# Ordering an edge list by block only, and placing its words by indirect DMA instead of by one-hot products

## The reference

```python
x = _layernorm(x + L0(x, edge_index_t, 1250, W, b))        # relu(x[src] W1 + x[dst] W2 + b), summed over edges by src
x = _layernorm(x + L1(x, edge_index, edge_type_8, edge_weight, ...))  # attention over edges, summed by dst
x = _layernorm(x + L2(x, src, dst, deg, ...))               # mean of x[src] by dst, then two products
x = _layernorm(x + L3(x, edge_index, edge_type_2, basis1, att1, ...)) # two gated layers, summed by src
```

## Time and profile before

| | |
|---|---|
| time of the runs | 2698.16 us median of 3 (2689.44 to 2699.32) |
| profiled execution, first to last instruction | 2541.8 us; its whole time is not recorded apart, the median is 156.4 us above this span |
| PE busy | 1969.9 us (78%) |
| DVE busy | 1458.9 us (57%) |
| POOL busy | 976.5 us (38%) |
| ACT busy | 479.5 us (19%) |
| DMA over the span | 336.66 MB, mean 132 GB/s |
| mean granted clock of PE | 0.883 |

### The profile page before, as it was taken

The page is one execution under the profiler, slowest core; times in us unless marked ns, Lnnn a source line. Parts: engine busy times, 40 slices in busy tenths (PEclk is TensorE's granted clock), DMA queues, the critical chain, the costliest instruction groups (busy, mean ns, idle before and its releaser), DMA issues. The chain is left out here.

```text
span 2541.8 us, 36616 instructions
## 1 busy us (share of the span) xinstructions
PE 1969.9 (78%) x8289; PEld 1126.0 (44%) x8290; DVE 1458.9 (57%) x3550; ACT 479.5 (19%) x889; POOL 976.5 (38%) x974
## 2 busy tenths in 40 slices
PE   7767695885989998558287775699867998888884
PEld 6633385564545554347144442233333333343331
DVE  5644467675257776687677777444453444204445
ACT  4101130111135554223200002100044000120000
POOL 0000000001047771440078773477700777207773
PEclk9988755998989999755599998899989999999998
DMA  0079700998046663000166670577712777317775
GB/s 16 0 160 212 157 0 21 205 206 214 32 117 193 186 191 74 26 0 0 50 176 172 173 183 28 174 208 210 196 36 95 236 209 207 102 66 206 209 208 143
DMA packets 99747, 336.66 MB, mean 132 GB/s; under 512 B 19744, under 2 KB 20369, under 8 KB 95851
## 3 DMA queue, kind: packets, MB, share of 16 engines
q0 software_dynamic: 71904, 235.41, 33.2%
q1 hardware_dynamic: 24714, 96.39, 14.9%
q10 hardware_dynamic: 3072, 4.20, 0.8%
HBM read 310.83 MB, written 25.10 MB: 132 GB/s over the span
## 5 line engine op out<-in xcount | busy, mean ns | idle before, releaser
L658 PE MATMUL e_pS<-e_rows,e_onehot_ring 128*128 128x512 f32 x1408 | 689.4, 617 | 179.9 <-issue 59.7
L578 POOL DMA_INDIRECT e_rows<-tab_y,e_idx_ring x352 | 334.8, 951 | 332.7 <-ACT e_idx_ring L638 226.1
L658 PEld LDWEIGHTS e_pS<-e_rows,e_onehot_ring 128*128 128x128 f32 x1408 | 246.4, 192 | 480.8 <-issue 404.6
L610 DVE TENSOR_TENSOR acc<-e_pS,acc 128x512 f32 x352 | 242.6, 689 | 377.1 <-PE e_pS L658 373.9
L578 POOL DMA_INDIRECT e_rows<-tab_h,e_idx_ring x176 | 205.0, 1165 | 208.1 <-ACT e_idx_ring L638 158.5
L968 PE MATMUL n_pY<-weights,n_xT_block 128*128 128x512 f32 x560 | 260.1, 615 | 0.0
L1583 POOL DMA_DIRECT2D a_in<-in_L_gnn_a_src x1 | 1.0, 966 | 611.0 <-POOLq L43 611.0
L578 POOL DMA_INDIRECT e_rows<-tab_n,e_idx_ring x176 | 167.7, 953 | 77.2 <-issue 49.9
L717 POOL DMA_INDIRECT e_rows<-tab_q,e_idx_ring x176 | 169.8, 965 | 68.1 <-issue 46.4
L792 PE MATMUL e_pS<-e_rows,e_onehot_f 128*128 128x512 f32 x352 | 166.6, 597 | 0.0
L968 PEld LDWEIGHTS n_pY<-weights,n_xT_block 128*128 128x128 f32 x560 | 107.5, 199 | 118.3 <-issue 118.3
(11 more groups left out here) (309 smaller groups left out, 3077.4 us busy)
## 6 DMA issues: line engine op xcount, KB each, us to landing
basis_piece<-in_L_gnn_basis SPq DMA_DIRECT2D x128, 480.0 KB, 11.8
tab_y<-n_y_ring SPq DMA_DIRECT2D x40, 256.0 KB, 2.2
e_rows<-tab_y,e_idx_ring POOLq DMA_INDIRECT x352, 3.7
tab_w<-basis_wout ACTq DMA_DIRECT2D x128, 32.0 KB
w_raw<-in_L_gnn_W SPq DMA_DIRECT2D x3, 1024.0 KB, 10.1
weights<-tab_w SPq DMA_DIRECT2D x3, 1024.0 KB, 5.8
e_rows<-tab_q,e_idx_ring POOLq DMA_INDIRECT x176, 3.7
e_rows<-tab_h,e_idx_ring POOLq DMA_INDIRECT x176, 3.8
```

Of the source, the lines that this page charges most:

```text
L578: pool.indirect_dma_start(rows[:, q, s, :], None, table, bass.IndirectOffsetOnAxis(idxr[:, half, n:n + 1], 0)).then_inc(got[q], 16)
L610: nc.vector.tensor_tensor(a, pS[:, u % 4, :], a, ALU.add).then_inc(added, 1)
L658: ins = nc.tensor.matmul(pS[:, u % 4, :], ohr[:, u % 4, s, :], rows[:, u, s, :], start=s == 0, stop=s == 1)
```

## The change

The source list alone is treated anew; the destination list is sorted and placed as before, by `sort_edges` (now without its third stage) and `place_edges` (that third stage as a function of its own, unchanged, with the tiles `pos_p`, `pos_s` and `value` passed in).

```diff
-            sort_edges(nc, "src", C, identb, f(SRC), [(f(DST), 1 << SH1), (f(REL1), 1 << SH2)], None,
-                       pairs["src"][:, :], blocks["src"][:, :], [packed["src"][:, :]], basis[1])
-            sort_edges(nc, "dst", C, identb, f(DST), [(f(SRC), 1 << SH1), (f(T8), 1 << SH2)], f(WT),
-                       pairs["dst"][:, :], blocks["dst"][:, :], [packed["dst"][:, :], weight[:, :]], basis[0])
+            pos_p, pos_s, value = (sb(n, [EP, T], F32)[:, :] for n in ("pos_partition", "pos_slot", "packed_value"))
+            bucket_edges(nc, "src", C, f(SRC), [(f(DST), 1 << SH1), (f(REL1), 1 << SH2)],
+                         pairs["src"][:, :], blocks["src"][:, :], pos_p, pos_s, value)
+            scatter_edges(nc, "src", C, pos_p, pos_s, value, dram("slots_src", [P * SLOTS, 1]), packed["src"][:, :], basis[1])
+            sort_edges(nc, "dst", C, identb, f(DST), [(f(SRC), 1 << SH1), (f(T8), 1 << SH2)],
+                       pairs["dst"][:, :], blocks["dst"][:, :], pos_p, pos_s, value)
+            place_edges(nc, "dst", C, pos_p, pos_s, value, f(WT), [packed["dst"][:, :], weight[:, :]], basis[0])
```

More of the change, by code:

```diff
@@ L234, in store, with sort_edges @@
             act.wait_ge(self.stored[k], self.STEPS * 64)
-def sort_edges(nc, name, C, identb, key, packed, extra, pair_block, block_f, sorted_out, basis=None):
-    values = [0] if extra is None else [0, 1]
+def sort_edges(nc, name, C, identb, key, packed, pair_block, block_f, pos_p, pos_s, value):
     with ExitStack() as ctx:
@@ L262, in sort_edges @@
         eqtmp = sb("eq_tmp", [EP, 4, EP], F32)
-        pos_p, pos_s = sb("pos_partition", [EP, T], F32), sb("pos_slot", [EP, T], F32)
-        value = sb("packed_value", [EP, T], F32)
         with ExitStack() as c1:
@@ L455, in _ @@
                 peeled(pe, T // GT // 2, step)
[L459 to L465, removed]
-            if basis:
[L467 to L517, removed]
@@ new lines, in scatter_edges, with _, step @@
+def scatter_edges(nc, name, C, pos_p, pos_s, value, slots, sorted_out, basis):
+    with ExitStack() as ctx:
+        sb = lambda n, s, d: ctx.enter_context(nc.sbuf_tensor(f"{name}_{n}", s, d))
+        sem = stage_semaphores(nc, ctx, name)
+        at = sb("slot_row", [EP, T], I32)
+        empty = sb("empty", [P, SLOTS], F32)
+        basis.begin(ctx, sem)
+        cleared, addressed, emptied, placed, read_back = (
+            sem("cleared"), sem("addressed"), sem("emptied"), sem("placed"), sem("read_back"))
+        block = ctx.enter_context(nc.Block())
+        by_part = slots.rearrange("(p s) a -> p (s a)", s=SLOTS)
+        @block.sync
+        def _(sp):
+            basis.load(sp)
+        @block.scalar
+        def _(act):
+            basis.store(act)
+        @block.vector
+        def _(v):
+            basis.clear_mix()
+            nc.vector.memset(empty[:, :], 0.0).then_inc(cleared, 1)
+            nc.vector.scalar_tensor_tensor(at[:, :], pos_p, float(SLOTS), pos_s, ALU.mult, ALU.add
+                                           ).then_inc(addressed, 1)
+        @block.gpsimd
+        def _(pool):
+            pool.wait_ge(cleared, 1)
[8 more added lines that the diff above has]
+            pool.wait_ge(read_back, 16)
+        @block.tensor
+        def _(pe):
+            basis.start_multiply(pe)
+            def step(i):
+                for k in range(2):
+                    basis.multiply(pe, i, k)
+            peeled(pe, Basis.STEPS, step)
```

115 lines of the change are left out of this document (111 added, 4 removed).

## The result

The change makes the kernel slower, by 0.6%: 2707.68 us median of 10 runs (2703.04 to 2714.21) against 2691.24 (2685.13 to 2702.54) of before, a ratio of 1.0058, 95% interval [1.0042, 1.0074]. Forecast were 2631.2 us and a range of 2590 to 2700. The profiled execution took 2704.2 us, its span 2701.9.

What follows compares the result with a forecast made beforehand. Stages follow one another across barriers, so a change is worth what it does to its own stage's length. Sorting -106.6 and placing +39.6 give -67.0 us: 2698.2 becomes 2631.2 us, range 2590 to 2700.

Steps and rivals of the forecast that it cites:

- Sort stage: Source list's sort: 126.75 us go, a DVE chain of 20.1 us takes their place, a saving of 106.6 us.
- The doubt about strides: Source list's sort: were the strided reduction and two strided products twice as slow, 26 us instead of 20.1.
- The rival of an unshortened stage: Source list's sort not shortened, through far slower strided operations; it would take 80 us more than 20; chance 0.03.
- The placing stage: Placing of the source list: POOL's chain of scatters takes 212.3 us against 172.7, or +39.6.
- I take 1.25, since a scatter too is one index for each partition: Placing of the source list: 160 scatters start 1.25 us apart, like gathers of 128 rows, 200 us in all.
- The upper bound of the text: Placing of the source list: scatters priced like gathers from `tab_h`, made while DVE multiplies rows, 1.47 us each, 235 us.
- This costs nothing if POOL may run ahead: Placing: scatters slowed to 4.4 us beside basis loads cost nothing; POOL issues all in 200 us, the rest drains behind.
- Hidden: Placing: without the 0.30 us of issue, scatters take 164 us under the basis work; 2592 us; chance 0.12.
- The engines become the bound: Placing: basis's 161 us plus 1250 words at 0.06 us make 248 us; 2667 us in all; chance 0.18.
- the cover of 0.034: Placing: POOL's pace of 200 us covers a cost of 0.034 us a word on a DMA engine.
- POOL held by a full queue: Placing: scatters slowed beside loads, the rest following at 1.25 us; 2708 us at 2.4 us each, 2746 at 4.4; chance 0.17.
- The list's order: Later gathers by the source list, whose rows now come in ascending destination order with repeats: costed at nothing.

Runs made afterwards that it cites:

- block order alone: The change with the source list's words placed by one-hot products instead of scatters: 2426.34 us, ratio 0.9561 to before; in a later job 2592.73 us, 0.9605.
- e2: Not a run but a later pass of the kernel; in the trace of before its 176 gathers of 128 rows show no gap above 0.31 us.
- the waits after 13: The change with POOL made to wait, after every 13 scatters, until all issued have landed: 2743.26 us (before: 2693.56 us in that job).
- 128-row version: The change with scatters of 128 rows instead of 125, the extra words going to spare places behind the table: 2486.41 us, ratio 0.979; in another job 2740.11 us, 1.0152.
- e0: Not a run but a pass of the kernel that gathers by the source list; its gathers of 128 rows stop before the 114th.

## Why the prediction was wrong

**Sort stage.** Right. 126.75 became 21.23 us, a saving of 105.5 where 106.6 was forecast. The doubt about strides was in place, but small. Two reductions of the kernel after:

```profile
22.77 2.83 DVE L513 TENSOR_REDUCE src_bucket<-src_in_bucket 125x160 f32<-125x1600 f32 x1
...
28.05 1.92 DVE L523 TENSOR_REDUCE block_of_pair_src<-src_pair_at_least 128x88 f32<-128x792 f32 x1
```

They were costed at 2.14 and 1.1 us. Both read with a stride and add up few terms for each result (10 and 9), and no run parts the two. The rival of an unshortened stage falls.

**The placing stage** was forecast at 212.3 us and took 294.8. By the forecast's own terms:

| term | forecast | measured | off |
|---|---|---|---|
| start to the first scatter | 4.0 | 3.2 | -0.8 |
| 160 scatters at their pace | 160 x 1.25 = 200 | 160 x 1.485 = 237.6 | +37.6 |
| POOL standing still | 0 | 50.1, less 4 x 0.3 of usual gap | +48.9 |
| last landing, read-back, barrier | 8.3 | 5.3 | -3.0 |

The measured is 34.06 less 30.91 for the start and 325.70 less 320.4 for the end. The terms sum to +82.7; 82.5 is what is to be explained.

**The first failed step is "I take 1.25, since a scatter too is one index for each partition".** The gap of 0.30 us was right to the hundredth, but POOL's own part is 0.97 us at 128 rows, 1.18 at 125 and 1.31 at 124. It rises with the words of a packet (8, 25 and 31, as worked out above), though not in proportion, and the gather from which the price came had 128 rows. The upper bound of the text, 1.47 us from the gathers of `tab_h`, was nearly the value, for another reason. By an estimate, at 1.485 us and with no stop the stage would have been 294.8 - 48.9 = 245.9 us, 73.2 above that of before, and the kernel 105.5 - 73.2 = 32.3 us faster.

**The second is "This costs nothing if POOL may run ahead".** It may for 39 scatters of 125 rows and for 113 of 128, and there are 160. The forecast has 0 us for POOL standing still, a term that no row and no run shows; with 125 rows the profile showed 50.1 us in four stops, and even with 128 rows POOL stopped once, for 12.96 and 20.37 us beside loads (206 to 210 GB/s until 155 us). The nine plain DMAs of the earlier trace rows were too few to show it, as the prediction said itself, but the trace of before had the row at 883.81 us, a stop of 1.95 us before the 114th gather, and the prediction did not use it.

**Rivals.** *Hidden* is refuted: the gap of 0.30 us stands throughout. *The engines become the bound* is refuted: scattering alone, from 275 to 320 us, the share is 0.07 at one scatter in 1.49 us, so a word costs, by an estimate from these, 0.07 x 16 x 1.49 / 125 = 0.013 us, under the cover of 0.034. The scatters did slow the loads: PE's last basis product ends at 217.3 us, 186.4 after the stage's start, where it took 167.7 before (305.1 - 137.4). These 19 us are not on the path, since POOL works 103 us longer. *POOL held by a full queue* was right in kind, and its 2708 us is by chance the result; its mechanism was not. It had POOL held at the engines' pace all through the loads. In fact POOL goes at its own pace and then stands still, which fits a wait until what is in flight has landed: with idle engines a stop of 2.3 us is the 1.6 to 1.7 us of a plain wait for landing and 0.65 more. The price of being held was 48.9 us, where the rival's 2708 us contained 289 - 212 = 77; the dearer scatter made up the rest.

**Costed at nothing.** The list's order is right by the block order alone. That PE's longer idle time costs the destination sort nothing is also a term that no row of before shows; it is right by the run, with 124.30 us at a granted clock of 0.50 against 124.05 at 0.51. The 156.4 us between span and median were wrongly taken for time around the span, but carried over unchanged they did no harm to the difference.

What is open: why the gathers of e2 and of `tab_y` run past 113 without a stop, and why a landing beside 16 KB packets costs 9.5 us and 0.35 us a scatter. With 8 KB packets the stops after 39 are 9.08 and 10.0 us instead of 20.23 and 23.14, and a backlog that only grows by the scatter would have made the waits after 13 a third of those after 39, which were 21.19 and 24.28 us where the waits were 12.6 to 15.0. How the DMA engines divide their time between the queues no run shows.

## What to carry to other kernels

Before replacing compute by many small DMAs, ask whether the compute was on the path: here the placing products lay under the basis loads, and the gain was in the other half of the change (0.956 to 0.9605 for block order alone). Price an indirect DMA at the row count that it will have: at 128 rows instead of 125 the same words cost 1.27 instead of 1.485 us each time and POOL stopped only after 113 of them instead of 39, though only the 128-row version held the loads back at the 2690 us level. Count how many indirect DMAs POOL issues in a row, landed or not: in these runs it stopped whole after 39 or 113, and beside large loads one such stop cost 9 to 24 us. Look for such a stop in the trace that is already there. And time a version in more than one job, as the 128-row version gained 2% in one and lost 1.5% in another.

## What the runs showed of the hardware

- POOL's time for an indirect DMA of one word a row: 0.969 us for 128 rows, 1.18 for 125, 1.31 for 124, with 0.30 us between any two.
- POOL stands still after 113, 39 and 31 of them. An estimate from these counts and from packets of 8, 25 and 31 words is a room of 1017 to 1023 places; no trace shows it. They are counted as issued since the last stop: with about two in flight (2.6 us to landing) the counts are the same. A stop takes 2.3 to 2.4 us with DMA engines 0.07 or 0.08 busy, 13 to 24 beside loads in runs of 16 KB at 178 to 210 GB/s, 8.6 to 10 beside runs of 8 KB at 181 to 213. The gathers of e0 show it too, with 1.95 us before the 114th in the trace of before; those of e2 and of `tab_y`, 176 in a row, do not.
- At the 2690 us level, and in neither job at 2542, runs of 128-row scatters went with an ACT and SP held back: the second half of a piece copied 25.7 us after PE had made it, 48 GB/s of loads instead of 208. The cause is open.
